# The positional softmax of the second layer moved from the expert stage into the token network and the relay stage

## What is computed

```python
patch_score = jax.nn.softmax(jnp.einsum('bhnd,bhmd->bhnm', q, k) * scale, axis=-1)
rel = _rel_indices(Nn)                  # stack of d, 0 and d * d, d = m - n
pos_score = (rel @ Wpos.T + bpos).transpose(2, 0, 1)
pos_score = jax.nn.softmax(pos_score, axis=-1)
g = jax.nn.sigmoid(gating)[None, :, None, None]
attn = (1.0 - g) * patch_score + g * pos_score[None]
attn = attn / attn.sum(axis=-1, keepdims=True)
```

## Time and profile before

| | |
|---|---|
| median of three | 729.44 us |
| the profiled execution, its own time | 727.95 us |
| its span, first to last instruction | 726.2 us |
| TensorE matmul busy | 600.5 us, 83% |
| VectorE busy | 444.4 us, 61% |
| GpSimd busy | 361.0 us, 50% |
| ScalarE busy | 277.9 us, 38% |
| TensorE's mean granted clock | 0.924 of full |

### The profile page before, as it was taken

The page is one execution under the profiler, slowest core; times in us unless marked ns, Lnnn a source line. Parts: engine busy times, 40 slices in busy tenths (PEclk is TensorE's granted clock), DMA queues, the critical chain, the costliest instruction groups (busy, mean ns, idle before and its releaser), DMA issues.

```text
span 726.2 us, 12294 instructions
## 1 busy us (share of the span) xinstructions
PE 600.5 (83%) x4657; PEld 473.8 (65%) x4657; DVE 444.4 (61%) x1099; ACT 277.9 (38%) x500; POOL 361.0 (50%) x402
## 2 busy tenths in 40 slices
PE   6889999998987706876887778666999698899996
PEld 3657777685556605766786767553688587785776
DVE  3644343337667736889789999985443726663534
ACT  0075354437976611211110100023733436566550
POOL 1696242217208636889889999346553300001334
PEclk9999999999999965889899999978998769999999
DMA  7000000000004330000000000000000000000000
GB/s 247 1 1 1 2 1 0 1 1 1 0 1 80 74 84 21 1 1 1 0 2 1 1 0 1 1 1 1 1 1 1 1 1 2 1 2 1 6 11 14
DMA packets 10698, 10.35 MB, mean 14 GB/s; under 512 B 5904, under 2 KB 9680, under 8 KB 10384
## 3 DMA queue, kind: packets, MB, share of 16 engines
q1 hardware_dynamic: 7936, 7.54, 3.7%
q0 software_dynamic: 1984, 1.62, 1.2%
q10 hardware_dynamic: 720, 0.41, 0.2%
HBM read 5.70 MB, written 0.52 MB: 9 GB/s over the span
## 4 chain that ended last, share of the span: by engine, by line
PE 56%; DVE 24%; ACT 7%; issue 5%; DMA 3%; POOL 3%; SPq 2%; ACTq 0%; DVEq 0%; POOLq 0%
PE bank L1071 8%; PE bank L1059 7%; DVE features L1774 6%; DVE bank L1808 5%; PE bank L1148 5%; DVE features L1797 5%; PE bank L1359 4%; PE bank L1322 4%; PE bank L1357 3%; PE bank L1423 2%; PE bank L1139 2%; PE bank L1411 2%; PE bank L1108 2%; PE bank L1117 2%; SPq L379 2%
## 5 line engine op out<-in xcount | busy, mean ns | idle before, releaser
L1148 PE MATMUL bank<-ident,features 128*128 128x128 f32 x920 | 127.0, 298 | 65.2 <-DVE features L1774 38.8
L1148 PEld LDWEIGHTS bank<-ident,features 128*128 128x128 f32 x920 | 114.0, 155 | 75.5 <-DVE features L1774 47.4
L506 POOL TENSOR_TENSOR features<-UV,coefs 128x1024 f32<-128x1024 f32 (+1 forms) x64 | 117.4, 1857 | 17.8 <-PE bank L1148 9.2
L1774 DVE TENSOR_TENSOR features<-UV,bank 128x1024 f32<-128x1024 f32 (+3 forms) x64 | 66.2, 1065 | 0.9
L695 ACT ACTIVATE G<-bank,cols 128x512 f32<-128x512 f32 x64 | 43.3, 686 | 49.6 <-PE bank L1059 49.6
L1059 PE MATMUL bank<-xs,weights 128*128 128x512 f32 x128 | 60.0, 614 | 2.5 <-ACT xs L686 2.5
L1071 PE MATMUL bank<-weights,G 128*128 128x128 f32 x512 | 59.8, 276 | 0.0
L1071 PEld LDWEIGHTS bank<-weights,G 128*128 128x128 f32 x512 | 58.4, 192 | 0.0
L349 POOL TENSOR_SCALAR rstd<-mv 128x4 f32<-128x4 f32 x8 | 1.9, 237 | 112.2 <-DVE mv L361 112.2
L762 ACT ACTIVATE hsT<-bank 128x256 f32<-128x256 f32 x16 | 6.1, 383 | 102.0 <-PE bank L1148 102.0
L481 POOL TENSOR_TENSOR UV<-xs,rows 128x512 f32<-128x512 f32 x16 | 20.3, 1270 | 46.8 <-DVE xs L1672 46.7
(11 more groups left out here) (318 smaller groups left out, 1346.2 us busy)
## 6 DMA issues: line engine op xcount, KB each, us to landing
weights<-in_w SPq DMA_DIRECT2D x2, 1024.0 KB, 11.6
features<-in_tok SPq DMA_DIRECT2D x1, 768.0 KB, 5.9
weights<-in_ew SPq DMA_DIRECT2D x4, 128.0 KB, 3.0
weights<-in_ew SPq DMA_DIRECT2D x2, 256.0 KB, 2.8
coefs<-G SPq DMA_DIRECT2D x16, 25.5 KB, 3.4
rows<-in_rows SPq DMA_DIRECT2D x1, 384.0 KB, 6.6
out_h<-H SPq DMA_DIRECT2D x3, 128.0 KB, 2.0
coefs<-G POOLq DMA_DIRECT2D x14, 25.5 KB, 4.9
```

Of the source, the lines that this page charges most:

```text
L506: pool.tensor_tensor(out, u, co, ALU.mult).then_inc(s["held_p"], 1)
L1148: last = mm(out[:, P * k:P * k + P], x[:, P * k:P * k + P], ident[:], is_transpose=True, start=first and k == 0, stop=last_ and k == n - 1 ...
L1774: dve.tensor_tensor(out, u, co.unsqueeze(3).broadcast_to([P, R, NH, DH]), ALU.mult)\
```

## The change

- `plog` lies in a new buffer `turns`, which also holds `dd` and `hsT`; `rel`, `rel2`, `rel_i` and `ptmp` lie in `SX`, and `posT` in the first 1024 columns of `rows`.
- GpSimd's steps become `positions(w)`, called behind `rstd_pool` of each unit from 4 on: units 4 to 9 have one step each. A wait for the last stands behind the loop.
- VectorE's offset moves behind `add(0)` in the token network, with a wait on the loads of the rows.
- VectorE's maximum, subtraction and softmax stand behind the last Gram copies, before `row_sums`.
- ScalarE's exponentials stand between its last relays and its `relayed`, and its two evictions behind `query_row(0)`.
- TensorE's eight transposes stand behind the last Gram products, into banks 0 and 1.

```diff
-        dd = sb("dd", [P, 2, HB])
+        turns = sb("turns", [P, 4 * HB])
+        dd = turns[:, 0:2 * HB].rearrange("p (k n) -> p k n", k=2)
-        hsT = sb("hsT", [P, 2, HB])
+        hsT = turns[:, 2 * HB:4 * HB].rearrange("p (k n) -> p k n", k=2)
-        ptmp = KKf[:, 0:1024].rearrange("p (h m) -> p h m", h=NH)
+        ptmp = SX[:, 2320:3344].rearrange("p (h m) -> p h m", h=NH)
-        posT = UVf[:, 6944:7968].rearrange("p (h n) -> p h n", h=NH)
-        plog = RKf[:, 0:1024].rearrange("p (h m) -> p h m", h=NH)
+        posT = rows[:, 0:1024].rearrange("p (h n) -> p h n", h=NH)
+        plog = turns[:].rearrange("p (h m) -> p h m", h=NH)
...
+            def positions(w):
+                if w == NC:
+                    ch(pool.iota(rel_i, pattern=[[1, P]], base=0, channel_multiplier=-1))
+                    ch.settle()
+                    ch(pool.tensor_copy(rel, rel_i))
+                elif w == NC + 1:
+                    ch.settle()
+                    ch(pool.tensor_tensor(rel2, rel, rel, ALU.mult))
+                elif w == NC + 2:
+                    ch(pool.tensor_tensor(plog, rel..., wp[:, 0]..., ALU.mult))
+                elif w == NC + 3:
+                    ch.settle()
+                    ch(pool.tensor_tensor(ptmp, rel2..., wp[:, 2]..., ALU.mult))
+                elif w == NC + 4:
+                    pool.wait_ge(s["p_offset"], 1)
+                    ch.settle()
+                    ch(pool.tensor_tensor(plog, plog, gate[:, 3, :]..., ALU.add))
+                elif w == NC + 5:
+                    ch.settle()
+                    pool.tensor_tensor(plog, plog, ptmp, ALU.add).then_inc(s["p_rel"], 1)
             for w in range(NC, NU):
                 prepare(w)
                 if w < 2 * NC:
                     pool.wait_ge(s["unit_first"], max(2, w - NC + 1))
                 rstd_pool(pool, ch, ("tok", w), CH)
+                positions(w)
+            pool.wait_ge(s["p_rel"], 1)
...
             for j in (6, 7):
                 relay(act, NG - 1, j)
+            act.activation(gate[:, 0, :], row("gating"), ACT.Exp, scale=-1.0).then_inc(s["gate_exp"], 1)
+            act.wait_ge(s["p_sub"], 1)
+            act.activation(plog, plog, ACT.Exp).then_inc(s["p_exp"], 1)
             for x in range(NS):
                 relayed(act, x, len(range(x, NG, NS)))
...
             query_row(0)
+            for k in range(2):
+                act.wait_ge(s["p_T"], k + 1)
+                act.activation(posT[:, 4 * k:4 * k + 4, :]..., bank[k][:], ACT.Copy).then_inc(s["p_evict"], 1)
             held_out(1)
...
             pe.wait_ge(s["gram_act"], 4 * NG)
             pe.wait_ge(s["gram_dve"], 4 * NG)
+            pe.wait_ge(s["p_done"], 1)
+            for k in range(2):
+                for j in range(4):
+                    last = nc.tensor.transpose(bank[k][:, P * j:P * j + P], plog[:, 4 * k + j, :], ident[:])
+                last.then_inc(s["p_T"], 1)
...
+            dve.wait_ge(s["load_rows"], 48)
             for w in range(NU - NC + 1):
                 add(w)
+                if w == 0:
+                    dve.scalar_tensor_tensor(out=gate[:, 3, :], ...).then_inc(s["p_offset"], 1)
...
             dve.wait_ge(s["gram_dve"], 4 * NG)
+            dve.wait_ge(s["p_rel"], 1)
+            ch(dve.tensor_reduce(comb[:, 0, 0:NH], plog, AX_X, ALU.max))
+            ch.settle()
+            dve.tensor_tensor(plog, plog, comb[:, 0, 0:NH]..., ALU.subtract).then_inc(s["p_sub"], 1)
             ch(dve.memset(bankER, 1.0))
+            positional_softmax()
             row_sums()
```

## The result

The changed kernel took 718.11 us, the median of four runs (717.11 to 719.37), beside 728.67 us (727.9 to 730.09) for the kernel before: a ratio of 0.9854, interval 0.9828 to 0.9879. The profiled execution took 717.5 us.

What follows compares the result with a forecast made beforehand. It took the engine ending the waits in each stage as the bound: VectorE's routing, then TensorE, in the expert stage. Gains of 3.70 us less 0.1 us made -3.6 us, from 729.44 to 725.8 us; range 722.5 to 728.6 us.

Steps and rivals of the forecast that it cites:

- Routing stalls: Expert stage: two VectorE routing steps no longer stalled beside GpSimd's instructions, a gain of 1.76 us.
- Table loads: Expert stage: ScalarE's exponential and two table loads leave, so TensorE's up-projections of chunk 2 gain 1.06 us.
- Transposes: Expert stage: eight transposes leave TensorE where it is the bound, 0.44 us for each four, a gain of 0.88 us.
- Token network: GpSimd's iota and cast may delay VectorE's apply of unit 4: cost 0.1 us, bounds 0 and 0.20 us.
- The 0.20 us: Token network: cost if VectorE's apply of unit 4 waits in full for GpSimd's iota and cast on the shared port.
- the cover named: Token network: unit 5's apply ends 3.2 us before its TensorE turn, later units at least that, so longer GpSimd steps cost nothing.
- Relay stage: The moved softmax chain fits VectorE's wait for the last transfer, with 1.4 us over: cost nothing.
- The short cover: Rival, relay stage: the softmax chain outlasts the relays or they land later; if later, 729.2 us; chance 0.12.
- two small rivals: Attention stage: one low clock stretch more, 732.3 us, chance 0.05; or one less, 719.3 us, chance 0.03.
- one stretch less: Rival, attention stage: one low stretch of the granted clock fewer, 719.3 us; chance 0.03.
- The last sentence of the prediction: Wrong if reciprocals follow VectorE's work, later token-network units slip, or low clock stretches move by more than the gain.
- The rival of the clock at 504 us: Expert stage: the clock stays up at the bias matmuls, another 2.6 us gained, 723.2 us; chance 0.12.

Runs made afterwards that it cites:

- no_logits: The kernel before without GpSimd's seven instructions that build the positional logits: 722.94 us, ratio 0.9924.
- no_exp: The kernel before with ScalarE's two exponentials of the positional part replaced by copies of 1 and 8 elements: 722.94 us, ratio 0.9932.
- tr_back: The changed kernel with eight dummy transposes put back behind the down-projections of chunks 1 and 2: 724.42 us, ratio to the kernel before 0.994.
- delay4: The changed kernel with four dummy VectorE reductions in the first routing steps, as a pure delay: 729.25 us, ratio to the kernel before 1.002.
- a_again: The changed kernel, unchanged, run and profiled a second time: 720.38 us, ratio to the kernel before 0.9899.
- delay2: The changed kernel with two dummy VectorE reductions in the first routing steps, as a pure delay: 722.49 us, ratio to the kernel before 0.9944.
- delay3: The changed kernel with three dummy VectorE reductions in the first routing steps, as a pure delay: 721.75 us, ratio to the kernel before 0.9946.
- b_again: The kernel before, unchanged, run and profiled a second time: 730.0 us, ratio 1.0027.
- all_back: The changed kernel with routing reductions, an exponential with its table loads and eight transposes put back as dummy work: 726.05 us, ratio to the kernel before 0.9977.
- no_turns: The kernel before with the eight positional transposes replaced by two matmuls of one column: 725.3 us, ratio 0.9957.

## Why the prediction was wrong

- **Routing stalls, -1.76 us: right.** -1.78 us, and -1.79 us alone.
- **Table loads, -1.06 us: right.** -1.06 us, and -1.04 us alone. The price by what TensorE lacked (0.96 us of gap), rather than by the 3.6 us that left ScalarE, was the right one.
- **Transposes, -0.88 us: right.** 0.44 us for each four. Together -3.72 us for -3.70.
- **Token network, +0.1 us: nothing.** The iota and the cast did not hold up the apply; the four long steps did theirs, inside the cover named. The 0.20 us that the prediction drew from the Trainium skill (SBUF — State Buffer, "SBUF: two separate sides") were not lost. In the trace the apply began 0.07 us before the iota's end and 0.14 us ahead of the cast, so that even by that rule it had at most 0.07 us to wait, and apply and cast ran side by side at their old lengths (1.11 and 0.36 us), which the rule, if it held for this pair, would not have allowed. The square of 128x128, with two inputs, held nothing up either (apply 1.11 us); only the four steps over 128x1024 did. TensorE's turn of unit 4 stands at 63.26 us, 0.34 earlier than named, but as far behind the apply's start as before (1.55 and 1.56 us).
- **Relay stage, 0: right.** 3.1 us were over, not 1.4 (the mis-sized part of this term, without effect): VectorE could start 0.9 us earlier (256.34), its softmax took 264.03 - 259.94 = 4.1 us instead of 4.63, and the memset stands where ScalarE makes the exponential. The short cover didn't happen, nor did GpSimd's transfers land later.
- **The clock: the step that failed.** The sum holds no term for it, and the runs put it at -6.5 us of rest. It took the low stretches of the kernel before as fixed in number and length, and gave their change two small rivals. That of one stretch less gave 719.3 us, 1.2 us from the result, with a chance of 0.03 and outside the range. Its mechanism was right and its size came out by luck: it took away the whole stretch from 581 us on, where the runs show that stretch shorter by 10.2 us and the one before it by 3.4. (That the clock goes down twice in the attention stage was a misreading: it falls a third time at 628.8 us, for 3.4 us.) The last sentence of the prediction names what came true, low stretches that move by more than the gain, but gave it no weight: the rows showed 15 us at 0.54 with TensorE 14.50 us busy, and the whole low time of 42.8 us was never added up. Put against each other, low time and rest show the size of the term. With the direct parts taken out, 13.5 us less low time go with 6.5 us (after), 14.0 with 5.5 (`no_logits`), 13.5 with 5.7 (`no_exp`), and in `tr_back` and `delay4` 6.1 and 13.5 us more with 2.8 and 5.1: 0.4 to 0.5 of it. (The dummies got less for theirs, 8.2 us for 24.2 and 2.0 for 11.9, a part of it being paid for the dummies themselves.) The kernel before thus had, by estimate, some 17 to 21 us of such loss from 490 us on (0.4 to 0.5 of 42.8), and an edit that moves the pattern by a third outweighs all its direct parts. Which way it would go could not be read from the kernel before; that it could be large could.
- The rival of the clock at 504 us, the likelier of the two towards a larger gain, did not happen: the fall came (498.7 us) and the bias matmuls took 3.59 us for 3.78. But the clock was back up at 505.6 us, 3.3 us behind their start where it had been 5.4, and from the matmul behind the routing to the first down-projection 2.69 - 1.96 = 0.73 us came of that.

**What stays open.** Why the stretch at 581 us lasts 3.4 us in one kernel and 13.7 in the other. In the kernels where the first turn of scores started 8.4 to 9.1 us after the fall, the stretch around the scores was 10.2 us long (after, a_again, no_exp, delay2, delay3), and where it started 9.4 to 10.6 us after it, 13.7 us (before, b_again, all_back, no_turns, tr_back). But the stretch that follows is not tied to that: `tr_back` and `no_turns` have the long one and no stretch at 581 at all, and `delay4` has the stretch at 581 without the long one before it. And why single executions of `all_back`, `tr_back` and `no_turns` spread over 10 us is not shown, as only one of each was profiled; nor is what the short executions of the kernel before looked like.

## What to carry to other kernels

Before a forecast for a stage that TensorE bounds, add up the low stretches of the granted clock behind the edit: what they change by counts 0.4 to 0.5 of its length, with either sign (here 28.8 to 42.9 us of low time among the 13 profiles without dummies, some 6 us of rest), and the range has to hold that. To learn what an edit itself brings, hold the clock in both kernels with dummy matmuls in TensorE's waits and compare these, by landmarks as well as by the total, since dummies that outlast a wait cost time of their own (1.5 us here); and if the low stretches are long, dummies can pay for themselves. An operation is priced by what the engine that waited for it lacked, not by its length: all direct terms here were right to 0.1 us.

## What the runs showed of the hardware

- The clock fell at 557.1 us when TensorE had been busy 4.46 of the 5.1 us from 552 on, and the stretch from 582 to 594 stayed at 0.50 with TensorE 6.00 of 6 us busy, twice. In these rows high busy time did not go with the high level.
- In three profiled executions of the changed kernel, and in two of the kernel before, the stretches behind 490 us stand at the same places behind the start of the expert stage, within 0.2 us.
- A delay of 5.0 us in VectorE's small steps cost 10 us of rest; one of 3.7 us cost 3.6.
- Beside a two-input GpSimd instruction over 128x1024, VectorE's apply took 2.59 and 3.04 us instead of 1.11; beside an iota of 0.24 and a cast of 0.36 us it took 1.11.
- The exponential of the gate, the first of a new place in the program, needed no table load: it stands at 257.58 us with 0.21 us, behind ScalarE's last two transfers, and no load is in the timeline between them.
